# An AdaLN transformer layer on one core: which engine takes which scores out of PSUM

## The chip, the cores and the metric

The kernel runs on one core of a Trainium2 chip. The metric is the time of one execution on the device in microseconds (us); less is better. The kernel before takes 2026.73 us (median of 3 runs, 2026.36 to 2027.8).

## The reference

One layer works on x of 4096 tokens by 256 features, in float32. A small matrix product of a conditioning vector gives shifts, scales and gates (`sa, ca, ga, sb, cb, gb`). Then:

```
h = layernorm(x) * (1 + ca) + sa
q = h, per head of 16 features, times Wq        (16 heads; q serves as query, key and value)
scores = q q^T * 4                              (4096 x 4096 for each head)
attn = softmax(scores);  res = attn q
x = x + ga * (res Wp^T + bp)
h = layernorm(x) * (1 + cb) + sb
x = x + gb * (h + 0.5 * (silu((layernorm(h)*gamma + beta) W1 + b1) W2 + b2))
```

W1 and W2 are dequantized from integers. Nearly all of the elementwise work is the exponential of 16 x 4096 x 4096 scores.

## The kernel before, in words

A start phase loads x, normalizes it, computes q, splits it into two float16 parts and stores these to DRAM, from where keys and queries ("asks") are loaded back. It ends some 82 us after the start. A tail of some 55 us finishes the last 512 tokens. Between them lies the attention phase, which is where the change is.

**Work of the attention phase.** The queries go in 8 chunks of 512 tokens and the heads in 4 groups of 4, which makes 32 (chunk, group) passes, `gg`. In a pass there are 64 *pairs*. A pair is one head and two tiles of 128 keys: two float16 matmuls of 64 rows (L831) write 128 keys x 512 queries each, into two neighbouring PSUM banks. Six banks hold scores, so three pairs are in PSUM at a time (`S_RING` = 3); a *round* (`at`) is three pairs, i = 0, 1 and 2, and there are 683 rounds in all (the last has two pairs). The exponentials go to SBUF, into a ring of 12 pairs (`place(n)`, four rounds long).

**Engines in a round before.** ScalarE waits for pairs 0 and 1 and takes both from PSUM in one exponential of 2048 columns (L795). VectorE waits for pair 2 and copies it as it is to its place in SBUF (L1011); ScalarE then makes the exponential of this pair in place, 1024 columns (L800). The count `exps_done` goes up by one for each exponential, `copied` by one for each copy. Before TensorE writes a pair of the next round it waits, at that pair, for its banks: pairs 0 and 1 for the exponential of L795, pair 2 for the copy.

**Sums.** `weigh` (L842) multiplies the exponentials by the values (and by a column of ones, for the softmax's sum), four heads side by side in the array. One *unit* is one tile of keys for 4 heads (four matmuls, eight records in the trace), a *step* is two units and four pairs. At the first unit of a step TensorE waits until the exponential of the step's last pair is done, `exps_with(4j+3)`. `units(gg)` deals the units out: none in rounds 0 and 1 of a pass, then one or two a round, and the last two (30 and 31) in round 0 of the next pass. In round 1 of the next pass the sums are turned, and VectorE divides (`copy_sums` L982 and `divide` L988 and L993).

**Pieces.** From chunk 1 on, the projection and the feed-forward network of the chunk before are cut into 40 pieces. `plan()` puts one piece in each round that `places(gg)` names (mostly rounds with one unit) and, where these don't suffice, in 4 or 5 rounds of a chunk that have two units, 33 in all. A piece is the last thing that TensorE does in a round. VectorE takes its result (`after_piece`), and for 56 of them ScalarE makes a tanh (L789) in the round after.

**Order.** Each engine runs its instructions in the written order. TensorE in round `at`: the three pairs of scores, then the units, then a piece if there is one. ScalarE: L795, a tanh if there is one, L800. VectorE: the copy, `copy_sums` or `divide`, `finish_hidden`, `after_piece`, then the layer norms (`norms`, in rounds 8 and 12 to 20 of group 0 of a chunk), `base_of` and `add_bias`. SyncE reloads keys when the scores that used them are done.

Of the kernel before, what the change touches and what calls it, by code (L numbers as in the profile page):

```python
# [7 lines left out]
ACT = mybir.ActivationFunctionType  # L8
# [26 lines left out]
GROUPS = G * Q_GROUPS  # L35
STEPS = TILES // 2
PAIRS = STEPS * Q_HEADS
S_RING, P_RING, K_RING = 3, 12, 4
# [10 lines left out]
ROUNDS = -(-GROUPS * PAIRS // S_RING)  # L49
# [48 lines left out]
def exps_with(n):  # L98

    at, i = divmod(n, S_RING)  # L100
    return 2 * at + 1 + i // 2


class Scope:
# [15 lines left out]
def wait(eng, semaphore, value):  # L120

    if value > 0:
        eng.wait_ge(semaphore, value)
# [39 lines left out]
def adaln_layer(nc, x, wq_t, wp_t, bp, gamma, beta, fc1_q, fc1_s, fc1_b, fc2_q, fc2_s, fc2_b,  # L163
# [9 lines left out]
    with ctx:  # L173
# [537 lines left out]
        ps_scores = a.banks("scores", 2 * S_RING)  # L711
# [5 lines left out]
        def place(n, pairs=1):  # L717

            first = 2 * (n % P_RING)
            return probs[:, first:first + 2 * pairs, :]  # L720

        def place_free(eng, n):

            if n >= P_RING:
                eng.wait_ge(steps_done, (n - P_RING) // Q_HEADS + 1)
# [8 lines left out]
        with nc.Block() as block:  # L734
# [46 lines left out]
            @block.scalar  # L781
            def _(act):
                scale = ctx.enter_context(act.register("exp_scale"))
                act.reg_load(scale, exp_scale[0:1, 0:1].bitcast(I32))

                def tanh(o, f):
                    act.wait_ge(half_ready, FT * o + f + 1)
                    wait(act, hidden_ready, FT * o + f - 1)
                    act.activation(half_tanh[:, f % 2, :], half_in[:, f % 2, :], ACT.Tanh).then_inc(tanh_done, 1)  # L789

                for at in range(ROUNDS):
                    n = S_RING * at
                    act.wait_ge(scores_ready, n + 2)
                    place_free(act, n + 1)
                    act.activation(place(n, 2), ps_scores[:, 0:4, :], ACT.Exp, scale=scale).then_inc(exps_done, 1)  # L795
                    if at in TANH_IN:
                        tanh(*TANH_IN[at])
                    if at + 1 < ROUNDS:
                        act.wait_ge(copied, at + 1)
                        act.activation(place(n + 2), place(n + 2), ACT.Exp, scale=scale).then_inc(exps_done, 1)  # L800

                for half in range(2):
                    cols = slice(half * D, (half + 1) * D)
                    act.wait_ge(tail_turned, half + 1)
                    for k in range(DC):
                        act.activation(ffn_in[:, k, cols], ps_scores[:, 4, k * D:(k + 1) * D], ACT.Identity,  # L806
                                       bias=beta_col[:, k:k + 1], scale=gamma_col[:, k:k + 1]).then_inc(tail_in, 1)
                    for f in range(FT):
                        act.wait_ge(tail_up, FT * half + f + 1)
                        act.activation(hidden[:, f, cols], ps_scores[:, f % 4, 0:D], ACT.Silu, bias=b1_col[:, f:f + 1]).then_inc(tail_hidden, 1)  # L810

            @block.tensor
            def _(pe):
# [3 lines left out]
                def scores(n):  # L817
                    gg, p = divmod(n, PAIRS)
                    i = n % S_RING
                    c, group = divmod(gg, Q_GROUPS)  # L820
                    j, hq = divmod(p, Q_HEADS)
                    part = n // K_PAIRS
                    if n % K_PAIRS == 0:
                        pe.wait_ge(k_in[part % K_RING], FILL_K * (part // K_RING + 1))
                    if p == 0:
                        pe.wait_ge(q_in[group], FILL_Q + (FILL_Q + FILL_SHIFT) * c)
                    if n >= S_RING:
                        pe.wait_ge(copied, n // S_RING) if i == 2 else pe.wait_ge(exps_done, exps_with(n - S_RING))
                    for b in range(2):
                        rows, col = slice(64 * b, 64 * b + 64), (j % K_STEPS) * P  # L830
                        last = pe.matmul(ps_scores[:, 2 * i + b, :], keys[rows, part % K_RING, hq, col:col + P],  # L831
                                         asks[rows, group * Q_HEADS + hq, :], start=True, stop=True)
                    last.then_inc(scores_ready, 1)
# [92 lines left out]
                for gg in range(GROUPS):  # L926
                    for r, (begin, end) in enumerate(units(gg)):
                        at = FIRST[gg] + r
# [50 lines left out]
            def _(dve):  # L979
                def copy_sums(gg):  # L980
                    dve.wait_ge(steps_done, STEPS * (gg + 1))
                    dve.tensor_copy(sums_sb, ps_sums).then_inc(sums_copied, 1)  # L982

                def divide(gg):
                    c, group = divmod(gg, Q_GROUPS)
                    turned = ps_sums.rearrange("p (t h e) -> p t h e", t=GT, h=Q_HEADS)
                    dve.wait_ge(sums_turned, gg + 1)
                    dve.reciprocal(inverse, turned[:, :, :, E]).then_inc(inverse_ready, 1)  # L988
                    dve.wait_ge(inverse_ready, gg + 1)
                    if c > 0 and group == 0:  # L990
                        dve.wait_ge(att_turned, 2 * c)
                    cols = slice(group * Q_HEADS * E, (group + 1) * Q_HEADS * E)
                    dve.tensor_tensor(att[:, :, cols].rearrange("p t (h e) -> p t h e", h=Q_HEADS), turned[:, :, :, 0:E],  # L993
                                      inverse.unsqueeze(3).broadcast_to([P, GT, Q_HEADS, E]), ALU.mult).then_inc(group_done, 1)
# [13 lines left out]
                def copy_scores(n):  # L1008
                    dve.wait_ge(scores_ready, n + 1)
                    place_free(dve, n)  # L1010
                    dve.tensor_copy(place(n), ps_scores[:, 4:6, :]).then_inc(copied, 1)  # L1011

                def add_bias(o):
                    dve.wait_ge(xn_in, 16 * (o + 1))
                    dve.tensor_tensor(x_now, x_now, wide(bp_ga[:, :]), ALU.add).then_inc(xb_ready, 1)
# [86 lines left out]
                def finish_hidden(o, f):  # L1102
                    dve.wait_ge(tanh_done, FT * o + f + 1)
                    dve.scalar_tensor_tensor(out=hidden[:, f, :], in0=half_tanh[:, f % 2, :], scalar=1.0, in1=half_in[:, f % 2, :],  # L1104
                                             op0=ALU.add, op1=ALU.mult).then_inc(hidden_ready, 1)
# [7 lines left out]
                def after_piece(o, s):  # L1113

                    if TURN_ATT <= s < TURN_ATT + DC:
                        take_att(o, s - TURN_ATT, ps_out)
                    elif s in (PROJECT + 1, PROJECT + 3):
                        b = (s - PROJECT) // 2
                        residual(o, b, ps_out)
                    elif TURN_Z2 <= s < TURN_Z2 + DC:  # L1120
                        take_z2(o, s - TURN_Z2, ps_out)
                    elif UP <= s < UP + DC * FT and (s - UP) % DC == DC - 1:
                        take_up(o, (s - UP) // DC)
                    elif s in (DOWN + FT - 1, DOWN + 2 * FT - 1):
                        finish_y(o, (s - DOWN) // FT, ps_out)
# [46 lines left out]
                for gg in range(GROUPS):  # L1172
                    c, group = divmod(gg, Q_GROUPS)
                    for r in range(FIRST[gg + 1] - FIRST[gg]):
                        at = FIRST[gg] + r
                        if at + 1 < ROUNDS:
                            copy_scores(S_RING * at + 2)
                        if r == 0 and gg > 0:
                            copy_sums(gg - 1)
                        if r == 1 and gg > 0:  # L1180
                            divide(gg - 1)
                        if at in HIDDEN_IN:
                            finish_hidden(*HIDDEN_IN[at])
                        if at in PIECE_IN:
                            after_piece(*PIECE_IN[at])
                        if c > 0 and group == 0:
                            norms(c - 1, r)
                        if c > 0 and group == 2 and r in (14, 16, 18):
                            base_of(c - 1, (r - 14) // 2)
                        if gg == 0 and 4 <= r < 8:  # L1190
                            modulation(r - 4)
                        if gg == 1 and 4 <= r < 12:
                            weights(r - 4)
                        if (group, r) == (3, 12):
                            add_bias(c)
# [81 lines left out]
```

## Time and profile before

| | |
|---|---|
| median of 3 runs | 2026.73 us |
| profiled execution | 2027.44 us |
| its span, first to last instruction | 2025.7 us |
| ScalarE busy | 1937.6 us, 96% |
| TensorE busy (matmul) | 1897.9 us, 94% |
| VectorE busy | 1192.9 us, 59% |

The span is read from the profile, whose engines are called PE (TensorE, matmuls), PEld (its weight loads), DVE (VectorE), ACT (ScalarE) and SP (SyncE). L795 is line 795 of the kernel before. A busy time counts instructions from start to end, and two neighbours on ACT or DVE can overlap a little; PE's ends are modelled. In rows that name a releaser, `<-`, the engine stood idle until that other instruction was done.

### The profile page before, as it was taken

The numbers are of one execution on the slowest core, as the hardware profiler recorded it, in microseconds if no ns is written. First come the engines' busy times: TensorE is split into PE (matmuls) and PEld (weight loads), VectorE is DVE, ScalarE is ACT, GpSimd is POOL, SyncE is SP. The second block draws the span as 40 slices with busy tenths as digits, with TensorE's granted clock in tenths as the row PEclk, the third lists the DMA queues.
The fourth block names the chain that finished last, engine by engine and source line by source line (L and its number), as shares of the span: only waits on it lengthen the run. The fifth ranks groups of instructions, "written<-read, shape, count | busy, mean of one in ns | idle before, by whom it ended". The sixth has DMA issues, their size and how long they took to land.

```text
span 2025.7 us, 43272 instructions
## 1 busy us (share of the span) xinstructions
PE 1897.9 (94%) x18477; PEld 550.7 (27%) x18477; DVE 1192.9 (59%) x1630; ACT 1937.6 (96%) x1491; POOL 1.3 (0%) x6
## 2 busy tenths in 40 slices
PE   6888889999999999999999999999999999999998
PEld 4411112222222222222222222222222222222225
DVE  7446445755576555755557555765557555576545
ACT  3899999999999999999999999999999999999982
POOL 0000000000000000000000000000000000000000
PEclk9999999999999999999999999999999999999999
DMA  5441111121112112111121211112121112111100
GB/s 163 135 145 39 44 51 42 46 57 43 49 45 51 53 43 62 45 43 48 52 52 45 58 42 50 44 51 52 43 61 46 40 50 57 48 37 45 33 12 12
DMA packets 121346, 108.14 MB, mean 53 GB/s; under 512 B 21936, under 2 KB 120112, under 8 KB 120896
## 3 DMA queue, kind: packets, MB, share of 16 engines
q1 hardware_dynamic: 120400, 103.69, 19.1%
q8 instruction: 146, 2.39, 0.5%
q10 hardware_dynamic: 752, 1.67, 0.2%
q14 instruction: 48, 0.39, 0.1%
HBM read 96.49 MB, written 8.65 MB: 52 GB/s over the span
## 4 chain that ended last, share of the span: by engine, by line
ACT 78%; issue 11%; PE 7%; DVE 1%; DVEq 0%
ACT attend_probs L795 42%; ACT attend_probs L800 34%; PE attend_sums L842 2%; PE attend_scores L831 2%; ACT attend_half_tanh L789 1%; PE attend_out L850 1%; PE attend_scores L850 1%; PE attend_scores L129 0%; DVE attend_probs L1011 0%; DVE attend_st L1029 0%; PE attend_sums L856 0%; DVE attend_x L1005 0%; ACT attend_ffn_in L806 0%; PE attend_scores L856 0%; DVE attend_mo L1036 0%
## 5 line engine op out<-in xcount | busy, mean ns | idle before, releaser
L795 ACT ACTIVATE attend_probs<-attend_scores 128x2048 f32<-128x2048 f32 x683 | 1322.5, 1936 | 3.4 <-PE attend_scores L831 3.2
L1011 DVE COPY attend_probs<-attend_scores 128x1024 f32<-128x1024 f32 x682 | 835.0, 1224 | 700.9 <-PE attend_scores L831 691.9
L842 PE MATMUL attend_sums<-attend_probs,values 128*17 128x512 f32 x8192 | 1006.6, 596 | 0.6 <-ACT attend_probs L795 0.3
L800 ACT ACTIVATE attend_probs<-attend_probs 128x1024 f32<-128x1024 f32 x682 | 763.5, 1119 | 1.2 <-DVE attend_probs L1011 1.2
L831 PE MATMUL attend_scores<-asks,keys 64*128 64x512 f16 x4096 | 562.2, 380 | 99.4 <-ACT attend_probs L795 73.5
L831 PEld LDWEIGHTS attend_scores<-asks,keys 64*128 64x128 f16 x4096 | 149.7, 94 | 711.0 <-ACT attend_probs L795 587.7
L842 PEld LDWEIGHTS attend_sums<-attend_probs,values 128*17 128x17 f32 x8192 | 173.9, 96 | 511.5 <-issue 459.2
L850 PE MATMUL attend_out<-w,hidden 128*32 128x256 f32 x1920 | 124.2, 379 | 0.0
L850 PE MATMUL attend_out<-attend_ffn_in,w 128*32 128x512 f32 x896 | 116.5, 592 | 0.0
L850 PEld LDWEIGHTS attend_out<-w,hidden 128*32 128x32 f32 x1920 | 62.0, 110 | 86.4 <-issue 64.3
L1100 DVE TENSOR_SCALAR attend_half_in<-attend_out,b_col 128x512 f32<-128x512 f32 x56 | 42.1, 751 | 16.3 <-PE attend_out L850 14.8
L850 PEld LDWEIGHTS attend_out<-attend_ffn_in,w 128*32 128x32 f32 x896 | 28.8, 110 | 64.2 <-issue 64.2
L1104 DVE SCALAR_TENSOR_TENSOR hidden<-attend_half_tanh,attend_half_in 128x512 f32<-128x512 f32 x56 | 38.2, 681 | 0.0
L982 DVE COPY attend_sums_sb<-attend_sums 128x512 f32<-128x512 f32 x32 | 22.1, 692 | 26.3 <-PE attend_sums L842 26.3
L789 ACT ACTIVATE attend_half_tanh<-attend_half_in 128x512 f32<-128x512 f32 x56 | 36.6, 653 | 0.0
L856 PE MATMUL attend_sums<-ident,attend_sums_sb 128*32 128x128 f32 x1024 | 34.6, 276 | 1.4 <-DVE attend_sums_sb L982 0.8
L401 ACT ACTIVATE start_h_feat<-start_ps,mod_col 128x512 f32<-128x512 f32 x16 | 11.5, 774 | 21.2 <-PE start_ps L449 21.2
L850 PE MATMUL attend_out<-wp,attend_att_feat 128*32 128x256 f32 x480 | 31.2, 379 | 0.0
L856 PEld LDWEIGHTS attend_sums<-ident,attend_sums_sb 128*32 128x32 f32 x1024 | 26.0, 109 | 16.5 <-DVE attend_sums_sb L982 16.5
L806 ACT ACTIVATE attend_ffn_in<-attend_scores,beta_col,gamma_col 128x256 f32<-128x256 f32 x4 | 2.0, 560 | 28.7 <-PE attend_scores L850 28.7
L850 PEld LDWEIGHTS attend_out<-wp,attend_att_feat 128*32 128x32 f32 x480 | 15.6, 110 | 22.6 <-issue 17.1
L471 PE MATMUL start_ps<-start_h_feat,start_wq_diag 128*128 128x512 f32 x32 | 17.0, 658 | 4.4 <-DVE start_q_parts L554 3.7
(145 smaller groups left out, 530.8 us busy)
## 6 DMA issues: line engine op xcount, KB each, us to landing
keys<-parts_dram SPq DMA_DIRECT2D x768, 64.0 KB
keys<-parts_dram SPq DMA_DIRECT2D x256, 56.0 KB
asks<-parts_dram SPq DMA_DIRECT2D x192, 64.0 KB
start_x_in<-L_attn_x SPq DMA_DIRECT2D x8, 512.0 KB, 9.5
parts_dram<-start_q_parts SPq DMA_DIRECT2D x16, 256.0 KB, 2.5
attend_x_now<-L_attn_x SPq DMA_DIRECT2D x8, 512.0 KB, 4.3
out<-base SPq DMA_DIRECT2D x16, 256.0 KB, 2.6
asks<-parts_dram SPq DMA_DIRECT2D x64, 56.0 KB
```

The source lines that it names most:

```text
L471: last = pe.matmul(ps_qf[:, k, :], wq_diag[:, k, :], h_feat[:, g % 2, k, :], start=True, stop=True)
L789: act.activation(half_tanh[:, f % 2, :], half_in[:, f % 2, :], ACT.Tanh).then_inc(tanh_done, 1)
L795: act.activation(place(n, 2), ps_scores[:, 0:4, :], ACT.Exp, scale=scale).then_inc(exps_done, 1)
L800: act.activation(place(n + 2), place(n + 2), ACT.Exp, scale=scale).then_inc(exps_done, 1)
L831: last = pe.matmul(ps_scores[:, 2 * i + b, :], keys[rows, part % K_RING, hq, col:col + P], asks[rows, group * Q_HEADS + hq, :], start=True ...
L842: last = pe.matmul(ps_sums[32 * hq:32 * hq + E1, :], values[:, j + STEPS * b, (gg % Q_GROUPS) * Q_HEADS + hq, :], place(gg * PAIRS + Q_HEA ...
L850: last = pe.matmul(to[32 * q:32 * q + 32, :], held[:, 32 * q:32 * q + 32], moved, start=start, stop=stop)
L856: last = pe.matmul(bank[32 * q:32 * q + 32, t * P:(t + 1) * P], source(t)[:, 32 * q:32 * q + 32], ident[:, :], start=True, stop=True)
L982: dve.tensor_copy(sums_sb, ps_sums).then_inc(sums_copied, 1)
L1011: dve.tensor_copy(place(n), ps_scores[:, 4:6, :]).then_inc(copied, 1)
L1100: dve.tensor_scalar(half_in[:, f % 2, :], ps_out, b1_col[:, f:f + 1], 0.5, ALU.add, ALU.mult).then_inc(half_ready, 1)
L1104: dve.scalar_tensor_tensor(out=hidden[:, f, :], in0=half_tanh[:, f % 2, :], scalar=1.0, in1=half_in[:, f % 2, :], op0=ALU.add, op1=ALU.mul ...
```

## The change

In a round, ScalarE takes pair 0 alone from PSUM, in one exponential of 1024 columns. VectorE copies pairs 1 and 2, in two copies of 1024 columns. ScalarE waits for both and makes their exponentials in place in one instruction of 2048 columns. The numbers of instructions on ScalarE and TensorE stay as they are; VectorE has 682 copies more. TensorE waits for the exponential before it writes pair 0 anew, and for the first and the second copy before pairs 1 and 2. `exps_with` changes with it: pair 1 now belongs to the second exponential of its round, so that a step whose last pair is a pair 1 waits for that one. In the last round, which has two pairs, pair 1 is copied as well. A tanh still lies between the two exponentials of its round.

```diff
 def exps_with(n):
     at, i = divmod(n, S_RING)
-    return 2 * at + 1 + i // 2
+    return 2 * at + 1 + min(i, 1)
+
+def copies_with(n):
+    at, i = divmod(n, S_RING)
+    return 2 * at + i
...
                 for at in range(ROUNDS):
                     n = S_RING * at
-                    act.wait_ge(scores_ready, n + 2)
-                    place_free(act, n + 1)
-                    act.activation(place(n, 2), ps_scores[:, 0:4, :], ACT.Exp, scale=scale).then_inc(exps_done, 1)
+                    copied_pairs = min(S_RING, GROUPS * PAIRS - n) - 1
+                    act.wait_ge(scores_ready, n + 1)
+                    place_free(act, n)
+                    act.activation(place(n), ps_scores[:, 0:2, :], ACT.Exp, scale=scale).then_inc(exps_done, 1)
                     if at in TANH_IN:
                         tanh(*TANH_IN[at])
-                    if at + 1 < ROUNDS:
-                        act.wait_ge(copied, at + 1)
-                        act.activation(place(n + 2), place(n + 2), ACT.Exp, scale=scale).then_inc(exps_done, 1)
+                    act.wait_ge(copied, copies_with(n + copied_pairs))
+                    act.activation(place(n + 1, copied_pairs), place(n + 1, copied_pairs), ACT.Exp, scale=scale).then_inc(exps_done, 1)
...
                     if n >= S_RING:
-                        pe.wait_ge(copied, n // S_RING) if i == 2 else pe.wait_ge(exps_done, exps_with(n - S_RING))
+                        pe.wait_ge(exps_done, exps_with(n - S_RING)) if i == 0 else pe.wait_ge(copied, copies_with(n - S_RING))
...
                 def copy_scores(n):
                     dve.wait_ge(scores_ready, n + 1)
                     place_free(dve, n)
-                    dve.tensor_copy(place(n), ps_scores[:, 4:6, :]).then_inc(copied, 1)
+                    dve.tensor_copy(place(n), ps_scores[:, 2 * (n % S_RING):2 * (n % S_RING) + 2, :]).then_inc(copied, 1)
...
-                        if at + 1 < ROUNDS:
-                            copy_scores(S_RING * at + 2)
+                        for n in range(S_RING * at + 1, min(S_RING * at + S_RING, GROUPS * PAIRS)):
+                            copy_scores(n)
```

## Rows read from the trace of the kernel before

**Rows 1.** The page: busy us (share of the span) and instructions.
```profile
PE 1897.9 (94%) x18477; PEld 550.7 (27%) x18477; DVE 1192.9 (59%) x1630; ACT 1937.6 (96%) x1491; POOL 1.3 (0%) x6
```

**Rows 2.** Windows: length, busy of PE, PEld, DVE, ACT, POOL, then PEclk.
```profile
82.56:1969.74 1887.18, 1787.81 (x17292) 473.96 (x17290) 1113.13 (x1359) 1884.33 (x1421) 0.00 (x0) 1.00 0.19 50
84.00:92.00 8.00, 5.96 (x30) 1.16 (x32) 2.45 (x2) 7.02 (x6) 0.00 (x0) 0.57 0.38 87
```

**Rows 3.** Timeline, two rounds: start us, length us, engine, line [idle before].
```profile
999.15 1.22 DVE L1011 COPY attend_probs<-attend_scores 128x1024 f32<-128x1024 f32 x1 [1.49 <-PE attend_scores L831]
1000.29 1.22 DVE L1015 TENSOR_TENSOR attend_x_now<-attend_x_now,bp_ga 128x1024 f32<-128x1024 f32 x1
...
1001.00 0.82 PE L831 MATMUL attend_scores<-asks,keys 64*128 64x512 f16 x6
1001.69 1.96 ACT L795 ACTIVATE attend_probs<-attend_scores 128x2048 f32<-128x2048 f32 x1
...
1003.45 1.15 ACT L800 ACTIVATE attend_probs<-attend_probs 128x1024 f32<-128x1024 f32 x1
...
1003.71 0.82 PE L831 MATMUL attend_scores<-asks,keys 64*128 64x512 f16 x6
1004.39 1.97 ACT L795 ACTIVATE attend_probs<-attend_scores 128x2048 f32<-128x2048 f32 x1
```

**Rows 4.** Timeline of the phase's first two rounds, where engines wait.
```profile
81.91 0.82 PE L831 MATMUL attend_scores<-asks,keys 64*128 64x512 f16 x6 [1.14 <-PEq L331]
82.56 1.88 ACT L795 ACTIVATE attend_probs<-attend_scores 128x2048 f32<-128x2048 f32 x1 [1.74 <-PE attend_scores L831]
...
84.33 1.05 ACT L800 ACTIVATE attend_probs<-attend_probs 128x1024 f32<-128x1024 f32 x1
```

**Rows 5.** Timeline of a stretch in which rounds with two units have a piece.
```profile
405.50 0.82 PE L831 MATMUL attend_scores<-asks,keys 64*128 64x512 f16 x6
...
406.14 1.88 ACT L795 ACTIVATE attend_probs<-attend_scores 128x2048 f32<-128x2048 f32 x1
...
407.12 1.04 PE L850 MATMUL attend_out<-attend_ffn_in,w 128*32 128x512 f32 x8
...
408.09 0.82 PE L831 MATMUL attend_scores<-asks,keys 64*128 64x512 f16 x6
...
408.84 1.91 PE L842 MATMUL attend_sums<-attend_probs,values 128*17 128x512 f32 x16
...
410.57 1.04 PE L850 MATMUL attend_out<-attend_ffn_in,w 128*32 128x512 f32 x8
...
411.55 0.82 PE L831 MATMUL attend_scores<-asks,keys 64*128 64x512 f16 x6
```

**Rows 6.** The page's groups: line engine operation, count | busy, mean ns | idle before, releaser.
```profile
L795 ACT ACTIVATE attend_probs<-attend_scores 128x2048 f32<-128x2048 f32 x683 | 1322.5, 1936 | 3.4 <-PE attend_scores L831 3.2
L1011 DVE COPY attend_probs<-attend_scores 128x1024 f32<-128x1024 f32 x682 | 835.0, 1224 | 700.9 <-PE attend_scores L831 691.9
L800 ACT ACTIVATE attend_probs<-attend_probs 128x1024 f32<-128x1024 f32 x682 | 763.5, 1119 | 1.2 <-DVE attend_probs L1011 1.2
```

**Rows 7.** Timeline of ScalarE with a tanh between its exponentials.
```profile
633.62 0.67 ACT L789 ACTIVATE attend_half_tanh<-attend_half_in 128x512 f32<-128x512 f32 x1
634.14 1.09 ACT L800 ACTIVATE attend_probs<-attend_probs 128x1024 f32<-128x1024 f32 x1
635.21 1.88 ACT L795 ACTIVATE attend_probs<-attend_scores 128x2048 f32<-128x2048 f32 x1
```

**Rows 8.** ScalarE's instructions of 1024 columns from PSUM in the start phase, by group.
```profile
L412 ACT ACTIVATE start_q_parts<-start_ps,gains 128x1024 f16<-128x1024 f32 x8 | 8.9, 1113 | 12.1 <-PE start_ps L471 12.1
...
L420 ACT ACTIVATE values<-start_ps 128x1024 f32<-128x1024 f32 x8 | 8.2, 1024 | 0.6 <-PE start_ps L483 0.3
```

**Rows 9.** Timeline at the end of the phase: VectorE's copy of sums, then TensorE.
```profile
1971.77 0.69 DVE L982 COPY attend_sums_sb<-attend_sums 128x512 f32<-128x512 f32 x1 [5.31 <-PE attend_sums L842]
...
1972.52 1.08 PE L856 MATMUL attend_sums<-ident,attend_sums_sb 128*32 128x128 f32 x32 [0.81 <-DVE attend_sums_sb L982]
```

**Rows 10.** Nine rounds with layer norms: window of VectorE, and its copies by group.
```profile
585.88:610.37 24.49, 21.69 (x59) 1.00 0.13 31
...
L1011 DVE COPY attend_probs<-attend_scores 128x1024 f32<-128x1024 f32 x9 | 11.0, 1223 | 1.8 <-PE attend_scores L831 1.7
```

**Rows 11.** VectorE's other instructions of 1024 columns, by group (first and last of six).
```profile
L1015 DVE TENSOR_TENSOR attend_x_now<-attend_x_now,bp_ga 128x1024 f32<-128x1024 f32 x8 | 9.7, 1216 | 0.0
...
L1165 DVE SCALAR_TENSOR_TENSOR w<-w,hidden 128x1024 f32<-128x1024 int32 x2 | 2.4, 1216 | 0.0
```

**Rows 12.** The page's chain that ended last: shares of the span by engine.
```profile
ACT 78%; issue 11%; PE 7%; DVE 1%; DVEq 0%
```

## The prediction

> **What bounds the kernel now.** I read the page's busy shares first [rows 1]: ScalarE 96%, TensorE 94%, VectorE 59%. The window over the attention phase is 1887.2 us long and ScalarE is busy in 1884.3 us of it, at TensorE's full clock [rows 2]. So 93% of the time is ScalarE's pace there, and whatever the change costs must appear as idle time of ScalarE. The timeline [rows 3] gives that pace: L795 starts at 1001.69, L800 at 1003.45, the next L795 at 1004.39, so 1.76 + 0.94 = 2.70 us a round. A second loop is as long: L795 ends (1001.69 + 1.96 = 1003.65), the scores start 0.06 later, and four matmuls after their start (0.65 us [rows 4]) the next L795 could go: 1.97 + 0.06 + 0.65 = 2.68. TensorE has 2.59 us of work in a round with one unit and a piece (405.50 to 408.09) and 3.46 in one with two units and a piece [rows 5]. The difference, 0.87, is a unit; so a round of two units and no piece takes 3.46 - 0.97 = 2.49, where 0.97 is the piece (407.12 to 408.09). VectorE idles 692 us waiting for scores [rows 6].
>
> **ScalarE's work doesn't change.** It still does 3072 columns a round in two instructions. 512 columns in place take 0.52 from start to next start [rows 7] and 1024 take 0.94 [rows 3], so another 512 cost 0.42. In place, 2048 columns then hold the engine 0.94 + 0.84 = 1.78, and end 1.05 + 0.84 = 1.89 after their start [rows 4]. Pair 0 from PSUM holds it 1.76 - 0.84 = 0.92 and ends after 1.88 - 0.84 = 1.04; other instructions of that size took 1.02 and 1.11 [rows 8]. Sum 0.92 + 1.78 = 2.70, as before. Bounds for the instruction of 2048 in place, which the trace lacks: 1.86 (as from PSUM) to 2.10 (twice 1.05); I take 1.89.
>
> **VectorE's work does.** 683 copies more (682 in the profile's count) of 1.22 us. A copy is followed by the next instruction 1.14 after its start (999.15 to 1000.29 [rows 3]), so two copies occupy 2.28 and are done 1.14 + 1.22 = 2.36 after the first starts. The trace has no two copies in a row, so 1.14 to 1.22 apart; I take 1.14. In total this fits: VectorE's other work in the phase is 1113 - 835 = 278 us [rows 2, 6], and 278 + 1365 x 1.14 = 1834 is under 1887. But it no longer fits everywhere, and it lies in a chain.
>
> By the Trainium skill, "VectorE: DVE Perf Modes", section "The DRAIN you can't avoid", the next VectorE instruction doesn't start until the pipe of the one before is empty. The trace here starts it 0.08 before the end of the copy. By the rule the two copies would take 2.44, and the sum below would be 0.04 x 683 = 27 us more, 2350.
>
> **The new chain.** TensorE writes its pairs in order, and pair 0 of round k waits for the exponential of pair 0 of round k-1. Pairs 1 and 2 stand behind it, though their banks are free earlier. Hence, from the start X of one exponential in place: 1.78 until the next round's pair 0 starts on ScalarE; 1.04 until it ends; 0.06 to the scores; 0.65 until pair 1 is readable (four matmuls); 1.14 + 1.22 for the copies; 0.06 to ScalarE (from VectorE to TensorE it is 0.06 [rows 9]). Sum 5.95, and that is the start of the exponential in place two rounds on. So 2.975 a round against ScalarE's 2.70: ScalarE waits 0.275 in each round for copies. 683 x 2.975 = 2032 against 1887: **+145 us**. The second loop above is gone, but nothing comes of it.
>
> **What comes on top.**
> - *Steps that end with pair 1 or 2.* When `weigh` begins a step whose last pair is pair 1 of the round before, that exponential was done before the scores of this round began. Now it ends 1.89 after X. Then 0.06, a unit (0.87) and a piece (0.97) follow before the next scores: X + 3.79, where the chain has the scores at X + 1.78 + 1.04 + 0.06 = 2.88. So 0.91 late. From `units` and `PIECE_IN`, 60 rounds have such a step's first unit and a piece: 55 us. At 20 of the 31 changes of pass, two units wait in the same way: 1.89 + 0.06 + 1.74 - 2.88 = 0.81, 16 us. Rounds without a piece lose under 0.1; left out.
> - *Layer norms.* Nine rounds took 24.49 us with VectorE idle before copies for 1.8 [rows 10]: 22.7 of occupation, plus 9 x 1.14 = 33.0, against 9 x 2.975 = 26.8. 6.2 x 7 chunks = 43 us.
> - *VectorE's single instructions of 1024 columns* (8 of L1015, 21 in `base_of`, 4 for weights [rows 11]): 2.28 + 1.14 - 2.975 = 0.445 each, 33 times: 15 us. Shorter ones (0.75 us for a piece) fit in the 0.69 that VectorE has left.
> - *Tanh*, 0.52 of ScalarE between the two exponentials [rows 7], of which the new idle time hides 0.275: 56 x 0.245 = 14 us.
> - *Two units and a piece without such a wait*, 14 rounds: 3.46 - 2.975 = 0.485, 7 us. The other 19 of 33 are in the 60.
> - *Last round*: a copy between two exponentials, 1 us.
>
> Sum 145 + 55 + 16 + 43 + 15 + 14 + 7 + 1 = 296 us. The profiled execution took 2027.44, which is 0.7 above the median; 2027 + 296 = 2323, and I give **2320**. Start and tail are untouched; SyncE's loads wait for scores and have more time.
>
> The unknowns: the chain could be 0.03 shorter, and delays on alternate rounds partly share (up to half of the 100 us of steps, pass changes, tanh and single instructions): 2240. Or copies 1.22 apart (0.08), 2048 columns in place holding 1.88 and pair 0 ending after 1.11: 0.25 more in two rounds, 85 us, and a little more: 2430.
>
> **Rivals.**
> 1. *VectorE as a mere load.* If its copies get a round ahead of ScalarE (the ring has four rounds of places, and a copy frees its banks at once), only stretches where it has more than 2.70 us of work lose: norms (33.0 - 24.5) x 7 = 60, single instructions (3.42 - 2.70) x 33 = 24: 2111. For it: the total of 1834 us. Against: the order on TensorE, pair 0 before 1 and 2. Chance 12%.
> 2. *Not slower.* As 1, and the norms' backlog is worked off from the ring too. Then ScalarE's own work is left, 683 x 2.70 + 56 x 0.52 = 1873, 14 us under today's 1887: 2013. It decides if no exponential in place ever waits for a copy. For it: the loop of 2.68, which today ties ScalarE to TensorE, is relaxed. Chance 4%. The Trainium skill, "TensorEngine Tiling (Array Packing)", section "PSUM Bottleneck", advises to share the emptying of PSUM between ScalarE and VectorE, and would speak for this one; ScalarE's columns, though, stay at 3072 a round.
> 3. *TensorE's clock falls.* In the phase's first rounds, with waits between scores, the granted clock was 0.57 [rows 2], about the lower of its two levels. TensorE's work in a round (2.5 us) would be 5.1 there. If it happened in one round in ten, 68 x (5.1 - 3.4) = 115 more: about 2440; with more rounds, far more. For it: TensorE would idle up to 1.3 us at a wait for the exponential in place. Against: a busy share over three quarters in every round. Chance 8%.
>
> **The numbers.** Forecast 76% (own range 2240 to 2430), rivals 12, 4 and 8%. The range 2170 to 2440 leaves out rival 1 and 2 and most of what lies past 3. A change under 0.2% (4 us) can't be told from none here: faster 2%, same 2%, slower 96%.
>
> **What would show it.** In the profile after, the exponential in place has a large idle time before it, released by VectorE's copy: 683 x 0.275 to about 0.4, some 190 to 290 us. Its mean is 1.9 to 2.0 us, the one from PSUM about 1.05. The chain of waits, 78% ScalarE and 1% VectorE now [rows 12], takes in copies with some 35 to 40% of the span. VectorE's busy share is near 2028 / 2320 = 87%. TensorE's `weigh` waits for the exponential in place at least 80 times. A plain round is 2.97 us, two rounds being equal in sum if not each, and the nine rounds with norms take 33 us. If the exponential in place starts without idle time in plain rounds, the chain is wrong and rival 1 holds; if `weigh` starts late but no time follows from it, the 71 us are.

## The result, and the profile after

The changed kernel takes 2309.9 us (median of 4 runs, 2307.87 to 2312.83) against 2027.26 us for the kernel before: 1.140 times as long, 95% interval 1.138 to 1.141. I had forecast 2320 us, slower, with 2170 to 2440 as the range.

The page of the changed kernel, busy time with share of the span and instructions, then shares of the chain of waits, then three groups as in [rows 6] (line numbers are those of the changed kernel: L802 is the exponential from PSUM, L806 the one in place, L1017 the copy, L848 `weigh`, L837 the scores, L856 a piece):

```profile
PE 1943.0 (84%) x18477; PEld 538.8 (23%) x18477; DVE 1938.6 (84%) x2313; ACT 1990.3 (86%) x1492; POOL 1.3 (0%) x6
...
DVE 30%; issue 30%; PE 19%; ACT 17%; DVEq 0%; ACTq 0%
...
L1017 DVE COPY attend_probs<-attend_scores 128x1024 f32<-128x1024 f32 x1365 | 1605.7, 1219 | 268.6 <-PE attend_scores L837 264.9
L806 ACT ACTIVATE attend_probs<-attend_probs 128x2048 f32<-128x2048 f32 (+1 forms) x683 | 1303.2, 1908 | 232.4 <-DVE attend_probs L1017 228.5
...
L802 ACT ACTIVATE attend_probs<-attend_scores 128x1024 f32<-128x1024 f32 x683 | 687.6, 1007 | 3.0 <-PE attend_scores L837 3.0
```

Where [rows 1] had ScalarE at 96% and VectorE at 59%, no engine now passes 86%: three engines, each busy five sixths of the time, and none of them the bound. The chain says the same: 78% ScalarE before [rows 12], and now 30% VectorE, 30% issue, 19% TensorE and 17% ScalarE. Two groups name the new wait. The exponential in place stood 228.5 us waiting for a copy, where L800 waited 1.2 us [rows 6], and the copy itself waited 264.9 us for scores. Waits in a ring, each engine for the next, are what a chain through several engines looks like. The list of waits (engine, line, whom it waited for: us in total, times, longest) shows the rest of the ring and `weigh`:

```profile
PE attend_scores L837 <- ACT attend_probs L802: 184.1, 309, 2.2
PE attend_sums L848 <- ACT attend_probs L806: 124.6, 132, 1.6
```

The attention phase, from the first exponential's start to the last one's end, is 2170.3 us long, against 1887.2 [rows 2]. That is 283 us more, the whole difference:

```profile
81.59:2251.85 2170.26, 1832.76 (x17294) 461.78 (x17290) 1858.84 (x2042) 1936.87 (x1422) 0.00 (x0) 0.99 0.16 44
```

ScalarE is idle there for 233 us (2170.3 - 1936.9), against 3 before. The other 53 us of the loss stand as more busy time (1936.9 against 1884.3), though the work is the same. Where ScalarE has to wait, two neighbours no longer overlap by their 0.1 us, and the overlap had counted once.

**The chain in one stretch without pieces.** Timeline of the changed kernel, start, length, engine:

```profile
271.06 1.90 ACT L806 ACTIVATE attend_probs<-attend_probs 128x2048 f32<-128x2048 f32 x1
271.22 0.82 PE L837 MATMUL attend_scores<-asks,keys 64*128 64x512 f16 x6 [0.61 <-ACT attend_probs L802]
...
272.86 1.02 ACT L802 ACTIVATE attend_probs<-attend_scores 128x1024 f32<-128x1024 f32 x1
273.93 0.82 PE L837 MATMUL attend_scores<-asks,keys 64*128 64x512 f16 x6
274.25 1.91 ACT L806 ACTIVATE attend_probs<-attend_probs 128x2048 f32<-128x2048 f32 x1 [0.38 <-DVE attend_probs L1017]
274.58 2.35 DVE L1017 COPY attend_probs<-attend_scores 128x1024 f32<-128x1024 f32 x2 [0.36 <-PE attend_scores L837]
...
276.97 1.91 ACT L806 ACTIVATE attend_probs<-attend_probs 128x2048 f32<-128x2048 f32 x1
```

Read it as the ring (the closed path of waits that the forecast calls the chain): the exponential in place starts at 271.06; 1.80 later (272.86) the next round's pair 0; it ends at 273.88, and the scores start 0.05 later; 0.65 after these, at 274.58, the copies, done at 276.93; and 0.04 later, at 276.97, the exponential in place of two rounds on. Sum 5.91; the forecast had 5.95. The two rounds are not alike, 3.19 and 2.72 (ScalarE's own 2.70 is the least), since the copies of odd and even rounds hang in two separate rings.

The same row shows two copies, x2, in 2.35: the second starts 1.13 to 1.14 after the first, before the first has ended, as assumed. The rule on the empty pipe that the forecast weighed (the Trainium skill, "VectorE: DVE Perf Modes", section "The DRAIN you can't avoid") would make it 2.44 if it held for every instruction. The forecast left out the end of the same paragraph: "A next op that is not held starts earlier". The copies here start earlier, as that sentence allows, and the measured 1.14 decides.

### The profile page after: what moved, and what is told of

It is laid out like the page before. It is cut to its first block, busy times and chain, and to the rows that moved or that the text cites. A ratio compares the mean times of both kernels' runs of the same rounds, so it can differ in the third digit from the quotient of the medians.

```text
span 2307.8 us, 44635 instructions
## 1 busy us (share of the span) xinstructions
PE 1943.0 (84%) x18477; PEld 538.8 (23%) x18477; DVE 1938.6 (84%) x2313; ACT 1990.3 (86%) x1492; POOL 1.3 (0%) x6
## 4 chain that ended last, share of the span: by engine, by line
DVE 30%; issue 30%; PE 19%; ACT 17%; DVEq 0%; ACTq 0%
DVE attend_probs L1017 25%; ACT attend_probs L806 10%; PE attend_sums L848 8%; ACT attend_probs L802 7%; PE attend_scores L837 7%; PE attend_out L856 3%; PE attend_scores L856 1%; DVE attend_st L1035 1%; DVE attend_half_in L1106 1%; DVE attend_hid L1057 0%; PE attend_scores L135 0%; DVE attend_sums_sb L988 0%; DVE hidden L1110 0%; DVE attend_hid L1062 0%; DVE attend_rsqrt_work L157 0%
## 5 line engine op out<-in xcount | busy, mean ns | idle before, releaser
L1017 DVE COPY attend_probs<-attend_scores 128x1024 f32<-128x1024 f32 x1365 | 1605.7, 1219 | 268.6 <-PE attend_scores L837 264.9
L806 ACT ACTIVATE attend_probs<-attend_probs 128x2048 f32<-128x2048 f32 (+1 forms) x683 | 1303.2, 1908 | 232.4 <-DVE attend_probs L1017 228.5
L848 PE MATMUL attend_sums<-attend_probs,values 128*17 128x512 f32 x8192 | 1034.5, 602 | 129.2 <-ACT attend_probs L806 124.6
L837 PE MATMUL attend_scores<-asks,keys 64*128 64x512 f16 x4096 | 582.8, 382 | 207.4 <-ACT attend_probs L802 184.1
L802 ACT ACTIVATE attend_probs<-attend_scores 128x1024 f32<-128x1024 f32 x683 | 687.6, 1007 | 3.0 <-PE attend_scores L837 3.0
L837 PEld LDWEIGHTS attend_scores<-asks,keys 64*128 64x128 f16 x4096 | 146.7, 94 | 884.1 <-ACT attend_probs L802 631.5
L848 PEld LDWEIGHTS attend_sums<-attend_probs,values 128*17 128x17 f32 x8192 | 164.7, 96 | 632.1 <-issue 355.1
L856 PE MATMUL attend_out<-w,hidden 128*32 128x256 f32 x1920 | 124.3, 379 | 0.0
L856 PE MATMUL attend_out<-attend_ffn_in,w 128*32 128x512 f32 x896 | 116.6, 592 | 0.0
L856 PEld LDWEIGHTS attend_out<-w,hidden 128*32 128x32 f32 x1920 | 62.1, 110 | 86.3 <-issue 64.2
L856 PEld LDWEIGHTS attend_out<-attend_ffn_in,w 128*32 128x32 f32 x896 | 28.9, 110 | 64.2 <-issue 64.2
L856 PE MATMUL attend_out<-wp,attend_att_feat 128*32 128x256 f32 x480 | 31.2, 379 | 0.0
L560 DVE SCALAR_TENSOR_TENSOR start_q_parts<-start_ps,gains,start_q_parts 128x1024 f16<-128x1024 f32 x8 | 10.3, 1284 | 14.9 <-ACT start_q_parts L418 14.8
L856 PEld LDWEIGHTS attend_out<-wp,attend_att_feat 128*32 128x32 f32 x480 | 15.6, 110 | 22.6 <-issue 17.1
```

Of the source, the lines that this page charges most:

```text
L802: act.activation(place(n), ps_scores[:, 0:2, :], ACT.Exp, scale=scale).then_inc(exps_done, 1)
L806: act.activation(place(n + 1, copied_pairs), place(n + 1, copied_pairs), ACT.Exp, scale=scale).then_inc(exps_done, 1)
L848: last = pe.matmul(ps_sums[32 * hq:32 * hq + E1, :], values[:, j + STEPS * b, (gg % Q_GROUPS) * Q_HEADS + hq, :], place(gg * PAIRS + Q_HEA ...
L856: last = pe.matmul(to[32 * q:32 * q + 32, :], held[:, 32 * q:32 * q + 32], moved, start=start, stop=stop)
L1017: dve.tensor_copy(place(n), ps_scores[:, 2 * (n % S_RING):2 * (n % S_RING) + 2, :]).then_inc(copied, 1)
```

## The experiments

All are timed against the kernel before on the same chip, where it took 2026.47 us (first four) or 2027.05 us (last three). Where I compare a *pass* (one of the 32, each of 21 or 22 rounds), its length runs from the start of its first exponential in place to that of the next pass.

### The same load on VectorE without the chain

```diff
# in the kernel before
                            copy_scores(S_RING * at + 2)
+                        idle_work(at)   # idle_out = ident * ident, 128x1024 in SBUF, waits for itself only
```

> The kernel before, with one more VectorE instruction of 1024 columns a round (a product in SBUF into a scratch tile that nobody reads), placed behind the copy of pair 2. VectorE then has the same load as after the change, but no step of the chain goes through the added work. Chain theory: only stretches in which VectorE has more than 2.70 us of work in a round lose, norms about 60 us and single instructions about 24 us: about 2111 us, and plain rounds stay at 2.71. Load theory (the change is slow because VectorE is as busy as 84% and the rest follows): about 2310 us, as the changed kernel.

Measured: 2111.46 us, ratio 1.043 (1.041 to 1.044). Its page, its waits and three rounds of its timeline:

```profile
PE 1910.5 (91%) x18477; PEld 550.2 (26%) x18477; DVE 1926.6 (91%) x2313; ACT 1956.0 (93%) x1491; POOL 1.3 (0%) x6
...
ACT attend_probs L803 <- DVE attend_probs L1019: 59.7, 110, 1.2
```

```profile
302.48 1.87 ACT L798 ACTIVATE attend_probs<-attend_scores 128x2048 f32<-128x2048 f32 x1
302.56 1.23 DVE L1019 COPY attend_probs<-attend_scores 128x1024 f32<-128x1024 f32 x1 [0.38 <-PE attend_scores L834]
303.70 1.22 DVE L1014 TENSOR_TENSOR attend_idle_out<-ident 128x1024 f32<-128x1024 f32 x1
...
305.18 1.87 ACT L798 ACTIVATE attend_probs<-attend_scores 128x2048 f32<-128x2048 f32 x1
...
307.89 1.88 ACT L798 ACTIVATE attend_probs<-attend_scores 128x2048 f32<-128x2048 f32 x1
```

VectorE does as many instructions as in the changed kernel (2313) and is busy nearly as long (1926.6 us against 1938.6, a larger share of a shorter span), yet plain rounds stay at 2.70 and the time grows by 85 us, not 283. This was rival 1's number to the microsecond, in a kernel where VectorE is indeed a mere load. That it is so exact is luck: the nine rounds with norms grew by 7.5 to 7.6 us each time, not by 8.5, and other rounds lost what is missing. If the two parts simply add, which no run shows, some 85 of the 283 us are VectorE's load in rounds where it is overfull. The other 200 or so need the order of the waits. A slowing of single instructions by the added traffic is not among the causes: in the changed kernel a copy takes 1219 ns against 1224 before [rows 6].

### The same work inside and outside the chain

```diff
# in the changed kernel; idle_work now has 256 columns
                         for n in range(S_RING * at + 1, min(S_RING * at + S_RING, GROUPS * PAIRS)):
                             copy_scores(n)
+                            if n == S_RING * at + 1: idle_work(at)      # between the copies
...
+                        idle_work(at)                                   # or: behind them
```

> The changed kernel with one more VectorE instruction of 256 columns a round (0.33 us to the next start, into a scratch tile), between the two copies. Chain theory: the second copy, and with it the exponential in place, is 0.33 later once in two rounds, 0.165 a round, about 113 us more, and some 10 us more in the rounds with norms: about 2430 us; plain rounds 3.14. Load theory: 0.33 in each round, 225 us: 2535.

> The same added instruction of 256 columns, but behind the second copy: the same load, outside the chain. Chain theory: it fits in the 0.69 us that VectorE has left in a plain round, which stays at 2.98; it costs 0.33 only in 63 rounds with norms and 33 with a single instruction of 1024 columns, about 32 us: about 2342 us. Load theory: no difference between this and the kernel with the work between the copies.

Measured: between 2459.92 us, ratio 1.214 (1.212 to 1.216); behind 2368.73 us, 1.169 (1.166 to 1.170). Against the changed kernel's 2309.9 that is +150 and +59, where I had expected +120 and +32. The difference between the two is what tells the theories apart: 91 us for one and the same instruction, by its place alone; I expected 88, and load alone predicts none. In pass 2, which has no pieces, 64.6 us became 64.6 with the work behind and 69.8 with it between. The ring itself shows it best. With the work between, two exponentials in place that are two rounds apart start 6.25 us apart, 3.125 a round for the 3.14 expected, where the changed kernel has 5.91:

```profile
256.48 1.91 ACT L809 ACTIVATE attend_probs<-attend_probs 128x2048 f32<-128x2048 f32 x1 [0.38 <-DVE attend_probs L1025]
...
262.73 1.91 ACT L809 ACTIVATE attend_probs<-attend_probs 128x2048 f32<-128x2048 f32 x1 [0.38 <-DVE attend_probs L1025]
```

In a stretch of the kernel with the work behind, the gap ahead of an exponential in place is what it was (0.37, against 0.38 in the stretch of the changed kernel above):

```profile
622.85 0.41 DVE L1020 TENSOR_TENSOR attend_idle_out<-ident 128x256 f32<-128x256 f32 x1
622.97 1.91 ACT L809 ACTIVATE attend_probs<-attend_probs 128x2048 f32<-128x2048 f32 x1 [0.37 <-DVE attend_probs L1025]
623.30 2.36 DVE L1025 COPY attend_probs<-attend_scores 128x1024 f32<-128x1024 f32 x2
...
625.69 1.91 ACT L809 ACTIVATE attend_probs<-attend_probs 128x2048 f32<-128x2048 f32 x1
```

The added instruction starts behind the second copy (622.85) and is out of the way when the next scores are readable. The two kernels took 30 and 27 us more than expected. With the work behind, passes with norms are 2.3 to 5.3 us longer each (expected 9 x 0.33 = 3.0), and the others -0.4 to 4.3. I had left out that short VectorE work, the copy of sums and the division fill part of the 0.69 us of slack. That this is where the 27 us went is an inference from the code; no run isolates it.

### The piece ahead of the units

```diff
# in the changed kernel, on TensorE
+                        if at in PIECE_IN:
+                            out_piece(*PIECE_IN[at])
                         for unit in range(begin, end):
                             weigh(gg, unit)
-                        if at in PIECE_IN:
-                            out_piece(*PIECE_IN[at])
```

> The changed kernel with the piece ahead of the units in each round that has one, on TensorE alone. My theory of the waits of weigh for the exponential in place: in the 60 rounds with such a wait the piece (0.97 us) now fills it, the scores of the next round are no longer 0.91 late, and about 55 us come back: about 2255 us; passes 6 and 18 fall from 3.20 to about 3.0 us a round. Rival: the waits cost nothing beside the chain, and the time stays at 2310.

Measured: 2288.42 us, ratio 1.129 (1.128 to 1.131), 21.5 us back and not 55. First the wait itself, in the changed kernel (the exponential in place started at 1101.46):

```profile
1101.46 1.91 ACT L806 ACTIVATE attend_probs<-attend_probs 128x2048 f32<-128x2048 f32 x1 [0.23 <-DVE attend_probs L1017]
...
1103.28 1.00 ACT L802 ACTIVATE attend_probs<-attend_scores 128x1024 f32<-128x1024 f32 x1
...
1103.42 1.05 PE L848 MATMUL attend_sums<-attend_probs,values 128*17 128x512 f32 x8 [1.31 <-ACT attend_probs L806]
...
1104.30 1.04 PE L856 MATMUL attend_out<-w,hidden 128*32 128x256 f32 x16
...
1105.27 0.82 PE L837 MATMUL attend_scores<-asks,keys 64*128 64x512 f16 x6
```

TensorE idles 1.31 us, then does its unit and its piece, and the scores start at 1105.27, though pair 0's exponential was done at 1104.28: 0.94 late beyond the usual 0.05, for the 0.91 of the forecast. Now the kernel with the piece first, one round that gained and one that lost:

```profile
704.49 1.07 PE L856 MATMUL attend_out<-attend_ffn_in,w 128*32 128x512 f32 x8
...
706.03 1.05 PE L848 MATMUL attend_sums<-attend_probs,values 128*17 128x512 f32 x8 [0.47 <-ACT attend_probs L806]
706.66 0.74 DVE L1106 TENSOR_SCALAR attend_half_in<-attend_out,b_col 128x512 f32<-128x512 f32 x1
...
714.00 0.74 DVE L1106 TENSOR_SCALAR attend_half_in<-attend_out,b_col 128x512 f32<-128x512 f32 x1
714.66 2.34 DVE L1017 COPY attend_probs<-attend_scores 128x1024 f32<-128x1024 f32 x2
714.80 1.06 PE L856 MATMUL attend_out<-attend_ffn_in,w 128*32 128x512 f32 x8 [0.78 <-DVE attend_half_in L1106]
```

At 704.49 the piece lies in the wait, of which 0.47 is left (1.31 in the round of the changed kernel above). Passes 6 and 18, with five such waits and no norms, fell by 4.2 us each, to 3.01 us a round, as expected: 0.84 a wait. But at 714.80 the piece itself waits 0.78, because VectorE takes the piece before it only behind its two copies. Passes 5, 8, 13, 17, 25 and 29 became 1.5 to 3.3 us longer. The mechanism holds; my expectation forgot what a piece moved forward would wait for.

### Pairs 1 and 2 ahead of pair 0

```diff
# in the changed kernel, on TensorE; the counts that others wait for are set to match
-                        for n in range(S_RING * at, min(S_RING * at + S_RING, GROUPS * PAIRS)):
+                        for n in [*pairs[1:], pairs[0]]:
                             scores(n)
```

> The changed kernel with the order of the pairs on TensorE changed to 1, 2, 0 (and the counts that ScalarE, VectorE and SyncE wait for set accordingly): the pairs that VectorE copies no longer stand behind pair 0's wait for its exponential. Chain theory: plain rounds fall from 2.97 to ScalarE's 2.71. What stays: VectorE's overload at norms and single instructions (as in the kernel before with the added load, 2111 us), and weigh's waits, now 6.58 against 5.40 for two rounds in 60 rounds with a piece (71 us) and about 22 us at the changes of pass: about 2204 us. If pair 0's wait is not what delays the copies: 2310.

> The same, and in each round the piece ahead of the units. The piece fills the wait of weigh, which should give back some 50 of the 71 us; pieces that wait for the product of the round before, which VectorE takes behind its two copies, lose about 20 us, as they did with the other order: about 2170 us.

Measured: 2241.07 us, ratio 1.105 (1.104 to 1.107), and with the piece first as well 2203.06 us, 1.087 (1.085 to 1.089). The order of three matmul pairs on TensorE gives back 69 us with no other work saved, so the copies did stand behind pair 0's wait. It gives less than the 106 I expected. Rounds without a wait of `weigh` are at 2.70 to 2.72, but those with one lose more than I had worked out, because the scores for the copies now follow `weigh` directly:

```profile
548.82 1.05 PE L853 MATMUL attend_sums<-attend_probs,values 128*17 128x512 f32 x8 [0.42 <-ACT attend_probs L806]
549.56 1.92 ACT L806 ACTIVATE attend_probs<-attend_probs 128x2048 f32<-128x2048 f32 x1
549.81 0.82 PE L842 MATMUL attend_scores<-asks,keys 64*128 64x512 f16 x6
550.24 2.36 DVE L1025 COPY attend_probs<-attend_scores 128x1024 f32<-128x1024 f32 x2 [0.97 <-PE attend_scores L842]
...
552.63 1.91 ACT L806 ACTIVATE attend_probs<-attend_probs 128x2048 f32<-128x2048 f32 x1 [0.24 <-DVE attend_probs L1025]
```

That is a round in which only the second unit waits, which I had put at under 0.1 for the changed kernel and left out here too. Here it makes the round 3.07 us (549.56 to 552.63) in place of 2.70, and there are 120 such places.

### Two exponentials in place, each behind its own copy

```diff
# in the changed kernel, on ScalarE; exps_with(n) becomes n + 1
-                    act.wait_ge(copied, copies_with(n + copied_pairs))
-                    act.activation(place(n + 1, copied_pairs), place(n + 1, copied_pairs), ACT.Exp, scale=scale).then_inc(exps_done, 1)
+                    for i in range(1, copied_pairs + 1):
+                        act.wait_ge(copied, copies_with(n + i))
+                        act.activation(place(n + i), place(n + i), ACT.Exp, scale=scale).then_inc(exps_done, 1)
```

> The changed kernel with two exponentials in place a round, each behind its own copy, in place of one behind both. Chain theory: the first one starts when the first copy is done, so from its start to the one two rounds on it is 1.14 (second copy) + 0.94 + 1.04 + 0.06 + 0.65 + 1.22 + 0.06 = 5.11, 2.56 a round, less than ScalarE's own 0.92 + 0.94 + 0.94 = 2.80. ScalarE becomes the bound again, at 2.80 in plain rounds, though it has one more instruction; weigh's waits go too. With the norms and single instructions as in the kernel before with the added load (2111 us) and some 60 us for the third instruction: about 2175 us. Load theory: VectorE's load is unchanged and ScalarE's larger, so 2310 or more.

Measured: 2153.88 us, ratio 1.062 (1.060 to 1.064). Its page, two waits, and two plain rounds:

```profile
PE 1934.1 (90%) x18477; PEld 548.1 (25%) x18477; DVE 1927.2 (90%) x2313; ACT 2020.2 (94%) x2174; POOL 1.3 (0%) x6
...
ACT attend_probs L807 <- DVE attend_probs L1018: 37.7, 83, 0.9
...
PE attend_sums L849 <- ACT attend_probs L807: 10.3, 11, 1.3
```

```profile
552.43 2.03 ACT L807 ACTIVATE attend_probs<-attend_probs 128x1024 f32<-128x1024 f32 x2
552.63 0.82 PE L838 MATMUL attend_scores<-asks,keys 64*128 64x512 f16 x6
553.28 2.35 DVE L1018 COPY attend_probs<-attend_scores 128x1024 f32<-128x1024 f32 x2 [0.36 <-PE attend_scores L838]
...
555.23 2.04 ACT L807 ACTIVATE attend_probs<-attend_probs 128x1024 f32<-128x1024 f32 x2
...
558.02 2.05 ACT L807 ACTIVATE attend_probs<-attend_probs 128x1024 f32<-128x1024 f32 x2
```

An instruction more on ScalarE in each round makes the changed kernel 156 us faster. The copies of a round run from 553.28, and the exponentials in place start at 555.23, when only the first is done; the period is 2.80 and 2.79, ScalarE's own, as worked out. ScalarE's wait for copies falls from 228.5 to 37.7 us, and that of `weigh` for the exponential in place from 124.6 to 10.3, since pair 1's exponential is now ready, and counted, by itself. So the single instruction of 2048 columns is the larger part of what the change costs, by both waits that it lengthens: ScalarE's for two copies, and TensorE's for its end. The run doesn't part the two. What remains against the kernel before, 127 us, would be the third instruction and VectorE's load; that is argued, not measured.

The lengths in us of some passes, side by side (first number: which pass; 3 has `add_bias` and no pieces, 6 has five waits of `weigh` ahead of a piece, 7 has `add_bias` and none of these, 16 has the norms):

```
pass  before  added load  changed  split exps  1,2 before 0  piece first
 3     59.6      60.3       65.6      62.4         62.5         65.6
 6     60.6      61.9       70.5      63.5         67.6         66.3
 7     56.9      57.7       63.1      59.1         59.4         63.5
16     57.6      66.2       69.3      66.4         67.4         69.5
```

No version beats the kernel before, and in all of them ScalarE still has to do 3072 columns in at least 2.70 us a round.

## Why the prediction was right

The sum was 296 us and the measured difference is 283, and the mechanism is the one forecast. That the two come so close is in part luck: several terms are off, in both directions. By its own steps:

- **ScalarE's work unchanged.** Right. The exponential in place took 1.908 us (1.89 taken), the one from PSUM 1.007 (1.04 taken), and a pair of them 2.72 where nothing waits. But the forecast said that all of the cost must appear as idle time of ScalarE, and 53 of the 283 us appeared as busy time.
- **The chain, 2.975 us a round, +145.** Right, and the step that the experiments test most: 65.6 us for the 22 rounds of pass 3 are 2.98 a round. The agreement to 0.01 is luck. The ring itself is 5.91 for two rounds, 2.955 a round, which over 683 rounds makes 14 us less. What lifts the mean again are things that the forecast left out, such as the waits of `weigh` in rounds without a piece (5.99 for the two rounds from 287.01, say), or booked elsewhere (the `add_bias` of this pass). Work put into the chain and outside of it, TensorE's order, and the split exponential each moved the time by the chain's rule in direction, and the two that were plainest (added load, split) within 22 us.
- **`weigh`'s waits ahead of a piece, 60 times 0.91.** The size nearly holds, 0.94 in the round shown. Pass 15 has five of them and is otherwise like pass 3 (22 rounds, `add_bias`, no tanh): (69.9 - 65.6) / 5 = 0.86. What comes back when one is filled is 0.84.
- **Norms, nine rounds in 33.0.** In pass 4 the first of them starts its exponential in place at 383.50 and the round behind them at 416.36: 32.86, against 24.49 before [rows 10]. In the other six chunks it is 32.1 to 33.8, so the term holds.
- **Single instructions of 1024 columns, 33 times 0.445, and tanh, 56 times 0.245.** Too dear, and the largest error. Passes 6, 10 and 14 each have two more single instructions and two more tanhs than passes 15, 7 and 11, to which they are otherwise alike. By the forecast that is 2 x 0.445 + 2 x 0.245 = 1.38 us; they are longer by 0.5 (70.5 against 69.9), 0.3 (63.5 against 63.1) and 0.0 (64.8 against 64.8). If the rest are like these, the two terms are worth some 6 us and not 29. Why they cost so little is not shown. A sharing of delays between the two rings, which the forecast put into its range, is one reading.
- **Changes of pass, 20 times 0.81.** Too cheap, where it can be read alone: at the end of pass 2 two rounds took 6.99 us, 1.08 over 5.91.
- **Two units and a piece without a wait, last round:** 8 us together, not measured by themselves.

These sizes don't add up to the 13 us exactly. The lower end of the forecast's own range is a slip besides: 2323 less 0.03 x 683 and half of 100 is some 2250, not 2240.

Of the signs announced, the wait for copies (228.5 us, forecast 190 to 290), the durations and `weigh`'s waits (132 on the matmuls, forecast at least 80) came as said. Two were off. The copies' share of the chain of waits was 25%, not 35 to 40; issue has 30% there, and a part of each link may be booked as that. VectorE's busy share was 84%, for the 87 forecast.

**The rivals.** Rival 1 describes the kernel with the added load and not the changed kernel. Rival 2 fell with it. Rival 3, the clock, is real and small. In rounds with norms the granted clock falls now and then, seven times in all; the kernel before has no such place behind its first rounds. Windows of the changed kernel (columns as in [rows 2]):

```profile
388.00:394.00 6.00, 3.90 (x34) 0.78 (x28) 5.74 (x13) 5.18 (x4) 0.00 (x0) 1.00 0.17 44
397.00:403.00 6.00, 5.40 (x32) 1.00 (x36) 5.96 (x11) 3.70 (x4) 0.00 (x0) 0.72 0.00 0
412.00:420.00 8.00, 6.09 (x64) 2.00 (x68) 6.11 (x9) 6.06 (x5) 0.00 (x0) 0.79 0.40 102
1214.00:1222.00 8.00, 6.00 (x38) 0.86 (x36) 7.96 (x14) 5.70 (x5) 0.00 (x0) 0.79 0.02 5
```

A mean of 0.72 means that the lower level, 1.2 GHz, was granted for a part of the window, right after TensorE had been busy 3.9 of 6 us. In windows of 4 us, 11 behind the first rounds lie under 0.95. What a fall costs is seen where the same work meets it or not: passes 4 and 5 (falls in the windows from 397 and from 412) took 138.9 us together, passes 16 and 17 (one fall, in the window from 1214) 137.0, and passes 28 and 29, which met none, 137.0 as well. So one fall cost nothing that can be seen and two cost 1.9 us, which makes a few us in all.

## What to carry to other kernels

Before work is moved to an engine that is idle 40% of the time, draw the ring that it closes: from one instruction through every wait back to the same instruction of a later round, and divide its length by the rounds that it spans. Here 5.95 us over two rounds, 2.975 a round, against 2.70 of the busiest engine gave half of the loss at once, while busy shares, 84 to 86% everywhere, would have called the kernel balanced. When such a ring binds, look for a wait that covers more than it needs (two copies where one would do, a matmul behind another's bank): splitting one instruction gave 156 us back though it added work.

## What the runs showed of the hardware

- VectorE starts an instruction behind a copy of 1024 float32 columns 1.13 to 1.14 us after the copy's start, though the copy takes 1.22. This holds also where a wait that is already met lies between them.
- ScalarE starts the next instruction 1.80 us after an in-place one of 2048 columns that takes 1.91, and two of 1024 cost some 0.09 us more than one of 2048 (2.80 against 2.70 to 2.72 a round).
- TensorE's granted clock, steady in the kernel before at over 94% busy, fell for a few microseconds at some places among the norms, where TensorE was busy 3.9 of 6 us, and not at the same places in every chunk. Single waits as long as there (1.55 us) stand elsewhere too, and no fall followed.
